# A Perceiver block on one core: the weighing of the values moves behind the step's value products

## The reference

```python
q = (query @ Wq + bq).reshape(b, sq, N_HEAD, KEY_DIM)
k = (key @ Wk + bk).reshape(b, key.shape[1], N_HEAD, KEY_DIM)
v = (value @ Wv + bv).reshape(b, value.shape[1], N_HEAD, VALUE_DIM)
scores = jnp.einsum('bqhd,bkhd->bhqk', q, k) / TEMP
attn = jax.nn.softmax(scores, axis=-1)
out = jnp.einsum('bhqk,bkhd->bqhd', attn, v).reshape(b, sq, N_HEAD * VALUE_DIM)
```

## Time and profile before

| what | value |
|---|---|
| median of 3 runs | 1759.67 us (1756.84 to 1759.78) |
| the profiled execution | 1760.32 us, span 1758.4 us |
| PE busy | 1597.2 us (91%) |
| DVE busy | 1289.3 us (73%) |
| ACT busy | 1009.3 us (57%) |
| POOL busy | 485.8 us (28%) |
| PE, 128 to 1000 us | 813.63 of 872.00 us busy, granted clock 1.00 |
| DVE, 128 to 1000 us | 727.20 us busy |
| ACT, 128 to 1000 us | 605.76 us busy |
| POOL, 128 to 1000 us | 264.84 us busy |

### The profile page before, as it was taken

How to read it: one execution, slowest core, us unless ns; L and a number is a source line. 1 busy time by engine, 2 the same in 40 slices (tenths; PEclk the granted TensorE clock), 3 DMA queues, 4 the chain that set the end, 5 groups by cost and what they waited for, 6 DMA issues and landing times. The chain is left out here.

```text
span 1758.4 us, 28297 instructions
## 1 busy us (share of the span) xinstructions
PE 1597.2 (91%) x10538; PEld 1326.2 (75%) x10538; DVE 1289.3 (73%) x2234; ACT 1009.3 (57%) x1966; POOL 485.8 (28%) x429
## 2 busy tenths in 40 slices
PE   6799999999999999999999887997599999999997
PEld 6677777777777777778777675775588888888886
DVE  3678888878887888888888766677668439548852
ACT  5557676777667666677676633443556336335641
POOL 2213332333232323322331043366501102102101
PEclk9999999999999999999999998998799999999899
DMA  6811462202120212011202571111847527527721
GB/s 230 281 62 31 75 125 67 64 10 66 63 67 7 67 61 67 10 64 61 67 13 78 168 242 48 43 60 56 283 146 238 150 85 233 153 96 210 224 61 21
DMA packets 80674, 182.58 MB, mean 104 GB/s; under 512 B 28596, under 2 KB 35124, under 8 KB 79968
## 3 DMA queue, kind: packets, MB, share of 16 engines
q1 hardware_dynamic: 61488, 140.79, 23.7%
q0 software_dynamic: 19024, 39.60, 9.6%
HBM read 152.48 MB, written 64.05 MB: 123 GB/s over the span
## 5 line engine op out<-in xcount | busy, mean ns | idle before, releaser
L507 PE MATMUL psum<-ctx,Wk 128*128 128x512 f32 x1536 | 386.2, 400 | 0.0
L507 PEld LDWEIGHTS psum<-ctx,Wk 128*128 128x128 f32 x1536 | 280.4, 189 | 55.8
L507 PE MATMUL psum<-xgT,Wh 128*128 128x224 f32 (+5 forms) x1536 | 250.1, 316 | 10.8 <-issue 10.8
L507 PEld LDWEIGHTS psum<-xgT,Wh 128*128 128x128 f32 x1536 | 228.2, 196 | 28.4 <-issue 13.4
L1553 ACT ACTIVATE Pr<-Pr,smn 128x512 f32<-128x512 f32 x128 | 92.7, 724 | 267.6 <-DVE smn L1120 267.6
L887 PE MATMUL psum<-Wh,hs 128*128 128x512 f32 x981 | 245.1, 395 | 0.3 <-DVE hs L1384 0.3
L1111 DVE SCALAR_TENSOR_TENSOR kT<-psum,bkc,kT 64x512 fp32r<-64x512 f32 x256 | 191.9, 750 | 71.4 <-ACT kT L1543 65.3
L887 PEld LDWEIGHTS psum<-Wh,hs 128*128 128x128 f32 x981 | 180.9, 190 | 34.3 <-DVE hs L1384 0.7
L1734 ACT ACTIVATE gl<-psum,b1c 128x512 f32<-128x512 f32 x128 | 87.7, 686 | 200.1 <-PE psum L507 200.0
L1118 DVE TENSOR_TENSOR Pr<-psum,Pr 64x512 f32<-64x512 f32 x256 | 176.3, 689 | 12.2 <-ACT Pr L1551 4.2
L1543 ACT ACTIVATE kT<-psum,bkc 64x512 fp32r<-64x512 f32 x256 | 174.1, 680 | 12.8 <-PE psum L507 9.4
(11 more groups left out here) (194 smaller groups left out, 2688.4 us busy)
## 6 DMA issues: line engine op xcount, KB each, us to landing
raw<-in_W SPq DMA_DIRECT2D x128, 512.0 KB, 3.8
raw<-in_ctxT SPq DMA_DIRECT2D x34, 512.0 KB
expert_rows<-in_spare_rows SPq DMA_DIRECT2D x16, 1042.0 KB, 8.7
xg<-expert_rows POOLq DMA_DIRECT2D x32, 256.0 KB, 5.1
q_rows<-qst POOLq DMA_DIRECT2D x16, 256.0 KB, 4.9
qb<-q_rows SPq DMA_DIRECT2D x16, 256.0 KB, 6.6
high_parts<-Ohr POOLq DMA_DIRECT2D x32, 128.0 KB, 3.9
low_parts<-Olo POOLq DMA_DIRECT2D x32, 128.0 KB, 4.5
```

Source lines behind the costliest of these rows:

```text
L507: mm = pe.matmul(dst, l, r, start=n == 0, stop=n == len(pairs) - 1)
```

## The change

In a step that has both, the weighing now stands behind the value products on PE, no longer between the scores and them. With it, the wait of `high_part(0)` and `high_part(1)` is for one product less (P4 of the last group in place of P5).

```diff
@@ -391,7 +391,7 @@
             def high_part(t):
 
                 if t < 2:
-                    sp.wait_ge(v_psum, 7 * NG - 1)
+                    sp.wait_ge(v_psum, 7 * NG - 2)
                     dst = oH[t][:]
                 else:
                     sp.wait_ge(k_psum, NS)
@@ -682,10 +682,10 @@
                     project_k(n)
                 if 0 <= n - 1 < NS:
                     scores(n - 1)
+                for G, name in v_products(n):
+                    project_v(G, name)
                 if n >= 6 and n % HALF == 2:
                     weigh(n // HALF - 1)
-                for G, name in v_products(n):
-                    project_v(G, name)
                 if 0 <= n - 2 < NS:
                     turn(n - 2)
                 if NS - 1 <= n <= NS + 1:
```

## The result

| | before | changed |
|---|---|---|
| median of 3 runs | 1759.67 us (1756.84 to 1759.78) | 1744.45 us (1744.39 to 1748.63) |
| profiled execution, span | 1760.32, 1758.4 us | 1744.39, 1742.6 us |
| start of `kT` high in step 3 and in step 127 | 109.03 and 997.42 us | 108.20 and 986.61 us |
| first and last Gelu of the experts | 1256.2 and 1738.7 us | 1244.9 and 1723.8 us |

The ratio is 0.9917, with a 95% interval of 0.9896 to 0.9938: 14.6 us faster (10.9 to 18.3). The forecast was 1750.8 us, 8.9 us faster, with a range of 1748.0 to 1758.0.

A forecast was written before the change was run, and what follows sets the result against it. The prediction took the ring of ACT and DVE, not PE, to bound the kernel. 14 x 0.61 = 8.5 us plus 0.4 made 8.9 us, giving a median of 1750.8 us, range 1748.0 to 1758.0.

The forecast's parts named there:

- Who sets the pace: From 128 to 1000 us, ACT and DVE set the pace and PE follows; shortening PE's list by itself buys nothing.
- POOL moves, the collision goes: POOL's L1791 starts about 3 us sooner, so L1794 misses DVE's scaling L1127, which falls from 1.57 to 0.49 us, 14 times.
- the ring: Loop of ACT and DVE: `kT` high, `kT` low, additions, maximum, exponential, PT, next `kT` high; turns without waiting for PE.
- PE must let the ring have it: PE's second key product after the weighing must end early enough for `kT` high to start 0.61 us sooner.
- the lead: PE reaches the turn 0.95 to 1.2 us earlier with the weighing moved back; without it only 1.7 us are gained.
- ACT's move of P1: ACT's L1522 must now await the weighing's end, 679.18 instead of 678.76; 1.07 us of cover, so nothing changes.
- the slower rival: POOL in its new place holds up DVE's additions and maximum, the ring losing 1.55 us 14 times: 1781.4 us; chance 0.04.
- The term 14 x 0.61 and the 0.4: Gain of 8.5 us from 14 collisions of POOL with DVE's scaling, plus ACT's one 0.4 us wait for PE.
- 0.61 us per collision give or take 0.1 is 1.4 us, and the three runs of before lie 2.9 us apart: Basis of the forecast's own range, 1748.5 to 1753 us, with chance 0.77.
- I see nothing that runs on a clock of its own: Stages behind the changed one start when it ends, so all of the 8.9 us should arrive.
- A measurement of this kernel can tell about 0.2%: Whole-kernel timing can tell about 3.5 us from no change.

The follow-up runs named there:

- e2: Changed kernel with POOL's L1791 held until the exponential of its step is done: 1757.85 us, ratio 0.9991 to the kernel before.
- e6: Kernel before with POOL's first low half of the sums (L1806) held until the scaling of Pr is done: 1751.34 us, ratio 0.9949.
- e3: Kernel before, weighing in its old place, with POOL's L1791 held until `Olo` is done: 1758.99 us, ratio 1.0001.
- e4: Kernel before with only SP's wait of `high_part` for one product less: 1758.99 us, ratio 1.0000.
- e1: The changed kernel again, no edit, nine runs: 1749.36 us, ratio 0.9953 to the kernel before.

## Why the prediction was right in its steps and wrong in its range

**Who sets the pace.** Right. Of the weighing's wait 34.7 us are gone and the stage is only 10.0 us shorter, 8.8 us of it at the 14 places where POOL met the scaling. e2 takes the gain back without touching PE, and e6 gains 8 us in the stage without touching it.

**POOL moves, the collision goes.** Right. L1791 moved by 3.48 us against the ring (about 3 forecast), L1127's sum fell by 15.7 us (15), and DVE waits for `kT` again.

**PE must let the ring have it.** Right, and the easiest step to leave out: 0.1 us per step without the lead was forecast (1.7 us in all) and e3 measured 0.11 (1.6 at the 14 places, 1.7 to 2.2 in the whole stage). The lead itself, 0.95 to 1.2 us in the forecast, was larger: the turn of step 82 starts 3.66 us behind the first `kT` high (671.80 against 668.14), where it was 5.03 (680.13 against 675.10), 1.37 us sooner. It was enough either way.

**ACT's move of P1** was not held up: DVE's wait for it is 46.0 us in both kernels. The additions and the maximum were not slowed by POOL, which was the slower rival.

**The term 14 x 0.61 and the 0.4.** The places are those forecast, and both terms were sized a little low. Read from one `kT` high to the next, the changed kernel gains 0.60 to 0.66 us at each of the 14 places, 8.8 us in all where 8.5 was forecast, and 0.53 in step 124 where 0.4 was. Another 0.25 us are two scalings beside POOL's transfers (L1826), which took 0.58 and 0.63 us before and 0.49 now. The 0.4 us that are left lie in hundredths all over the stage and are within the 0.49 us by which e4 differs from the kernel before.

**What failed** is the width of the range, in two steps. The first is "0.61 us per collision give or take 0.1 is 1.4 us, and the three runs of before lie 2.9 us apart". I took 2.9 us, the spread of three runs, for the spread of the measurement. 32 runs of the same kernel lie 14.6 us apart, and the first three runs of the changed kernel had a median 4.9 us under that of nine later ones (1744.45 and 1749.36). The second is "I see nothing that runs on a clock of its own": the stages outside the cross-attention stood in the sum at nothing, and the range gave them no width. They gave 5.8 of the 15.8 us between the first two profiles, 3.6 of them in the experts, where the granted clock of PE differed; e1 did not repeat those 3.6. So part of the first result was luck: the three runs of the changed kernel had mean clocks of 0.972 to 0.974, the nine of e1 0.970 on average. With the nine, the change measures 1749.36 us where 1750.8 was forecast, and 9.5 us of gain by medians where 8.9 was. "A measurement of this kernel can tell about 0.2%" describes one interval, which is 0.2% to either side here, but the two measurements of the change, 0.9917 and 0.9953, lie 0.36% apart.

## What to carry to other kernels

A wait on the busiest engine is worth what the ring that sets the pace can use of it; ask first whether anyone ever waits for that engine. When an instruction on a side engine is released by the one that is moved, look at what it will run beside in its new place: here this was nearly the whole gain, once PE was ahead, and one added wait that keeps POOL off DVE's scaling gave as much again. And a gain of half a per cent is read from the distance of two fixed instructions in the profile before it is read from the total: that distance repeated to 0.03 us in one pair of profiles and to 0.5 in another, while 32 runs of one kernel lay 15 us apart.

## What the runs showed of the hardware that I had not expected

The hold between POOL and DVE goes both ways, and a few hundredths of a microsecond decide its direction. Where POOL starts between 0.02 us ahead of the scaling and 0.03 us behind it (the 14 places of the kernel before; in step 82 both start at 681.82), the scaling takes 1.55 to 1.61 us; where POOL is 0.06 to 0.08 us behind (e2, in step 82 at 680.97 and 681.04) the scaling takes 0.49, POOL 1.56 instead of 1.29, and DVE's next instruction with two inputs in SBUF 1.97 us for a pair instead of 0.86. DVE's instructions with one input in PSUM (L1118) and its maximum (L1120) ran beside the same POOL instructions at 690 and 686 ns.

The granted clock of PE was 1.00 in the stretch from 128 to 1000 us in both kernels. In the experts it was below 1 in places and differed between executions of one kernel: 0.83 and 0.79 over the same 40 us of the changed kernel, where the whole of the experts took 478.9 and 482.6 us.
